# Graph layer with a sort on chip: five VectorE operations a sort stage, one stream of sort slots over three walks, sixteen one-hots and eight gather slots

## The reference, cut to what matters

```python
x   = x + gnn(layernorm(x), W, row=src, col=dst, vals=edge_weight)
x   = x + ffn(layernorm(x), W_ffn, b_ffn)
# gnn: h = x @ W.T ; out[row[e]] += vals[e] * h[col[e]]   for 131,072 edges
```

## Time and profile before

| | us |
|---|---|
| median of 3 runs (1778.59 to 1779.0) | 1778.88 |
| the profiled execution's own time | 1777.97 |
| its span, first to last instruction | 1776.2 |
| phase 1 / four walks / rest, cut at the first and the last gather | 278 / 1331 / 167 |
| busy in the whole span: PE, DVE, ACT, POOL | 1633.4, 1173.2, 604.1, 1065.1 |

### The profile page before, as it was taken

The page is one execution under the profiler, slowest core; times in us unless marked ns, Lnnn a source line. Parts: engine busy times, 40 slices in busy tenths (PEclk is TensorE's granted clock), DMA queues, the critical chain, the costliest instruction groups (busy, mean ns, idle before and its releaser), DMA issues.

```text
span 1776.2 us, 29342 instructions
## 1 busy us (share of the span) xinstructions
PE 1633.4 (92%) x4076; PEld 651.5 (37%) x4077; DVE 1173.2 (66%) x4540; ACT 604.1 (34%) x1354; POOL 1065.1 (60%) x1114
## 2 busy tenths in 40 slices
PE   7999997999999999999999999999999999995995
PEld 4455542433333423333333233333343333332442
DVE  7666656777777787778777877878743333335465
ACT  7777732222222222222222122222244444443341
POOL 1000005777777777777667677776777777775930
PEclk9999998999999999999999999999999999998798
DMA  7334215777777777766667676766677777772334
GB/s 256 119 133 136 91 68 167 212 209 207 209 206 207 209 207 204 203 198 196 191 191 202 189 202 192 203 193 188 192 209 210 209 209 210 210 209 64 131 111 140
DMA packets 121766, 323.92 MB, mean 182 GB/s; under 512 B 20434, under 2 KB 39154, under 8 KB 121586
## 3 DMA queue, kind: packets, MB, share of 16 engines
q0 software_dynamic: 81920, 268.50, 53.2%
q1 hardware_dynamic: 39666, 53.48, 8.9%
HBM read 288.35 MB, written 33.55 MB: 181 GB/s over the span
## 4 chain that ended last, share of the span: by engine, by line
PE 55%; DVE 16%; DMA 9%; issue 8%; POOL 7%; DVEq 3%; ACT 1%; SPq 1%; ACTq 0%; POOLq 0%
PE psum L1201 34%; PE psum L1109 12%; DMA region<-h_rows,region 9%; POOL region L519 7%; DVE region L918 5%; PE psum L1280 4%; DVEq L918 2%; DVE region L827 2%; DVE region L817 2%; PE psum L1098 2%; DVE region L821 1%; DVE region L829 1%; DVE region L831 1%; DVE region L823 1%; PE psum L1248 1%
## 5 line engine op out<-in xcount | busy, mean ns | idle before, releaser
L519 POOL DMA_INDIRECT region<-h_rows,region x1024 | 984.8, 962 | 615.9 <-DMA h_rows<-region 268.8
L1201 PE MATMUL psum<-region 128*128 x2552 | 1237.3, 617 | 84.2 <-DVE region L918 44.8
L1201 PEld LDWEIGHTS psum<-region 128*128 128x128 f32 x2552 | 433.3, 189 | 849.9 <-issue 845.7
L918 DVE SCALAR_TENSOR_TENSOR region<-region 128x128 f32 (+1 forms) x1276 | 450.5, 353 | 437.8 <-PE psum L1201 290.7
L679 ACT ACTIVATE x<-psum 128x512 f32<-128x512 f32 x192 | 114.6, 597 | 784.8 <-PE psum L1201 784.8
L1109 PE MATMUL psum<-region 128*128 128x512 f32 x512 | 230.2, 593 | 0.8 <-ACT region L581 0.8
L831 DVE COPY_PREDICATED region<-region 128x128 f32<-128x128 int32 x452 | 159.0, 352 | 0.0
L827 DVE COPY_PREDICATED region<-region 128x128 f32<-128x128 int32 x452 | 158.1, 350 | 0.0
L662 ACT ACTIVATE psum<-x 128x512 f32<-128x512 f32 x256 | 153.7, 601 | 8.0
L817 DVE TENSOR_TENSOR region<-region 128x128 int32<-128x128 f32 x452 | 130.4, 289 | 23.1 <-ACT region L608 21.5
L829 DVE TENSOR_TENSOR region<-region 128x128 f32<-128x128 f32 x452 | 136.4, 302 | 0.0
(11 more groups left out here) (150 smaller groups left out, 637.9 us busy)
## 6 DMA issues: line engine op xcount, KB each, us to landing
x<-in_x SPq DMA_DIRECT2D x16, 1024.0 KB, 6.1
h_rows<-region SPq DMA_DIRECT2D x64, 256.0 KB, 2.0
region<-h_rows,region POOLq DMA_INDIRECT x1024, 3.7
out<-x SPq DMA_DIRECT2D x4, 2816.0 KB, 10.8
out<-x SPq DMA_DIRECT2D x8, 640.0 KB, 3.4
region<-in_L_gnn_weight SPq DMA_DIRECT2D x1, 1024.0 KB, 5.5
region<-in_src SPq DMA_DIRECT2D x4, 128.0 KB, 2.5
region<-in_dst SPq DMA_DIRECT2D x4, 128.0 KB, 2.4
```

The source lines that it names most:

```text
L519: pool.indirect_dma_start(gathered[:, (c + 1) % RING, :], None, h_dram, bass.IndirectOffsetOnAxis(ap=dst_i[g][:, i:i + 1], axis=0),).then_ ...
L918: dve.scalar_tensor_tensor(spread[:, slot % SR, :], iota_n[:, bass.ds((tile - (g * T + 1)) * P, P)], src_f[g][:, bass.ds(chunk - (g * NC + ...
L1201: pe.matmul(banks[:, bass.ds(pe.snap(tile_wanted) % AGG, 1), :].rearrange("p t f -> p (t f)"), spread[:, slot % SR, :], gathered[:, bass.d ...
```

## The change

- A stage has five operations. Weights now alternate between two buffers too, `other_weights` and `weight[g]`. In the keys slot, **all** weights (256 columns) are copied to the other buffer in place of the low half, between compare and minimum. The weights slot is the maximum, then **one** predicated copy of 256 columns: mask broadcast over both halves, data read with the halves of each pair exchanged.
- "pack" copies the part's weights into `other_weights` first (one operation more).
- Where VectorE moves turned data (not ScalarE), only the keys are copied from PSUM. The first stage behind the turn reads the weights from PSUM directly; TensorE no longer waits for a copy of them.
- `plan()` has 0.65 for a keys and for a weights slot, before 0.6 and 0.85. Worked through, `HEAD` goes from slot 40 (17 whole stages of part 1) to slot 59 (26 stages), and every one of the 18 turns and sums of part 0 moves one tile of phase 1 earlier (the first from behind tile 9 to behind tile 8, with the same spacings after it).
- What is left of parts 1 to 3 is one list, spread evenly over steps 0 to 944 of 957; before, each walk had its own. A stage (keys 1.0, weights 0.9) gets 2.08 steps in every walk; before 2.16 in walk 0 and 1.91 in walks 1 and 2.
- `SR` 8 to 16, `RING` 11 to 8.

```diff
-    RING = 11
-    SR = 8
+    RING = 8
+    SR = 16
@@ plan
-        vector_times = {"pack": 6.0, "flip": 0.3, "keys": 0.6, "weights": 0.85, ...
+        vector_times = {"pack": 6.0, "flip": 0.3, "keys": 0.65, "weights": 0.65, ...
@@ slots_with_steps
+        left = [(g, slot) for g in range(1, PARTS) for slot in SORT_SLOTS[HEAD if g == 1 else 0:]]
+            return {"keys": 1.0, "weights": 0.9, "turned": 0.9, "flip": 0.4, "rest": 0.5}.get(what, 0.7)
+        room = ((PARTS - 1) * NS - LAST_STEPS) / sum(shares)
@@ sort_edges
+                        dve.tensor_copy(weights_now, weight[g]).then_inc(s_sort[g], 1)
...
-                        dve.tensor_copy(kept, low_w).then_inc(s_sort[g], 1)
+                        dve.tensor_copy(weights[1 - now], weights_now).then_inc(s_sort[g], 1)
                         dve.wait_ge(s_sort[g], done + 1)
                         dve.tensor_tensor(to_low, low, high, ALU.min).then_inc(s_sort[g], 1)
...
-                        dve.copy_predicated(low_w, swap, high_w).then_inc(s_sort[g], 1)
-                        dve.wait_ge(s_sort[g], done)
                         dve.tensor_tensor(to_high, low, high, ALU.max).then_inc(s_sort[g], 1)
-                        dve.wait_ge(s_sort[g], done + 1)
-                        dve.copy_predicated(high_w, swap, kept).then_inc(s_sort[g], 1)
+                        dve.wait_ge(s_sort[g], done)
+                        dve.copy_predicated(both(weights[1 - now], j),
+                                            swap.unsqueeze(2).to_broadcast(both(weights_now, j).shape),
+                                            both(weights_now, j)[:, :, ::-1, :]).then_inc(s_sort[g], 1)
...
-                            dve.tensor_copy(keys[now], turned_keys).then_inc(s_key_in[g], 1)
-                            dve.wait_ge(s_turn_w[g], turns)
-                            dve.tensor_copy(weight[g], turned_weights).then_inc(s_wgt_in[g], 1)
+                            weights_now = turned_weights
+                            dve.wait_ge(s_turn_k[g], turns)
+                            dve.tensor_copy(keys_now, turned_keys).then_inc(s_key_in[g], 1)
+                            dve.wait_ge(s_key_in[g], turns)
```

More of the change, by code:

```diff
@@ L101, in gnn_ffn @@
     assert sum(what == "turn" for what, _, _ in SORT_SLOTS) == TURNS
+    assert sum(what == "weights" for what, _, _ in SORT_SLOTS) % 2 == 1
     def plan():
-        vector_times = {"pack": 6.0, "flip": 0.3, "keys": 0.6, "weights": 0.85, "turned": 1.9, "maxima": 2.5,
+        vector_times = {"pack": 6.0, "flip": 0.3, "keys": 0.65, "weights": 0.65, "turned": 1.9, "maxima": 2.5,
                         "counts": 2.0, "rows": 2.0, "index": 0.4, "source": 0.8}
@@ L135, in gnn_ffn, with slots_with_steps, share @@
     HEAD_TURNS = sum(what == "turn" for what, _, _ in SORT_SLOTS[:HEAD])
[L137 to L145, removed]
+    def slots_with_steps():
+        left = [(g, slot) for g in range(1, PARTS) for slot in SORT_SLOTS[HEAD if g == 1 else 0:]]
+        def share(what):
+            return {"keys": 1.0, "weights": 0.9, "turned": 0.9, "flip": 0.4, "rest": 0.5}.get(what, 0.7)
+        shares = [share(what) for _, (what, _, _) in left]
+        room = ((PARTS - 1) * NS - LAST_STEPS) / sum(shares)
+        found, at = [0] * (PARTS * NS), 0.0
+        for (g, _), of_one in zip(left, shares):
+            step = int(at * room)
+            assert step < g * NS - LAST_STEPS
+            found[step] += 1
+            at += of_one
         return found
@@ L165, in gnn_ffn @@
         AT_SORT = AT_DATA + PARTS * 3 * NC
[L166 removed]
+        AT_TAB = AT_SORT + 4 * NC
         REGION = AT_TAB + NSP + NC + T
@@ L204, in gnn_ffn @@
         keys = [carve(NC), carve(NC)]
-        rest = carve(NC + NC // 2)
+        rest = carve(2 * NC)
         swaps = [rest[:, i * NC // 2:(i + 1) * NC // 2].bitcast(I32) for i in range(2)]
-        low_kept = rest[:, NC:NC + NC // 2]
-        below = low_kept
+        other_weights = rest[:, NC:2 * NC]
+        below = other_weights[:, 0:NC // P * T]
         over = rest[0:T, 0:NSP]
@@ L372, in row_of, with weights_of @@
             return slice(32 * g, 32 * g + 1)
-        SORT_STEPS = {"pack": 2, "flip": 1, "keys": 3, "weights": 3}
+        SORT_STEPS = {"pack": 3, "flip": 1, "keys": 3, "weights": 2}
+        BY_SCALAR = (TURNS, HEAD_TURNS) + (0,) * (PARTS - 2)
+        def weights_of(g):
+            return other_weights, weight[g]
         def progress(turn):
@@ L768, in sort_edges, with both @@
                 done = turns = now = half = 0
+                weights = weights_of(g)
+                keys_now, weights_now = keys[0], weights[0]
+                def both(a, j):
+                    return a.rearrange("p (b s d) -> p b s d", s=2, d=1 << (j if j < 7 else j - 7))
                 def pairs(a, j):
-                    v = a.rearrange("p (b s d) -> p b s d", s=2, d=1 << (j if j < 7 else j - 7))
-                    return v[:, :, 0, :], v[:, :, 1, :]
+                    return both(a, j)[:, :, 0, :], both(a, j)[:, :, 1, :]
                 def single(a, j):
@@ L810, in sort_edges @@
                     elif what == "keys":
-                        low, high = pairs(keys[now], j)
+                        low, high = pairs(keys_now, j)
                         to_low, to_high = pairs(keys[1 - now], j)
-                        low_w, high_w = pairs(weight[g], j)
                         swap = single(swaps[half], j)
-                        kept = single(low_kept, j)
                         dve.wait_ge(s_sort[g], done - 1)
                         dve.tensor_tensor(swap, low, high, ALU.is_gt).then_inc(s_sort[g], 1)
-                        if turns:
+                        if turns > BY_SCALAR[g]:
+                            dve.wait_ge(s_turn_w[g], turns)
+                        elif turns:
                             dve.wait_ge(s_wgt_in[g], turns)
                         dve.wait_ge(s_sort[g], done)
-                        dve.tensor_copy(kept, low_w).then_inc(s_sort[g], 1)
+                        dve.tensor_copy(weights[1 - now], weights_now).then_inc(s_sort[g], 1)
                         dve.wait_ge(s_sort[g], done + 1)
@@ L925, in _ @@
                 dve.wait_ge(s_hst[u], 16 * (T // 4))
[L926 to L934, removed]
+            following = chain(second, *[sort_edges(g) for g in range(2, PARTS)])
+            for at, slots in enumerate(slots_with_steps()):
+                build(*divmod(at, NS))
+                for _ in range(slots):
+                    next(following)
+                if at == SR:
+                    for cleared in (all_fwT, all_fw_in, bias.rearrange("p h l -> p (h l)"), fw_out[:, :]):
+                        dve.memset(cleared, 0.0).then_inc(s_fz, 1)
             go, = counters(dve, "dve_live")
@@ L1115, in turn_edges @@
                 pe.wait_ge(s_sort[g], steps - 1)
-                if turn or g:
-                    pe.wait_ge(s_key_in[g if turn else g - 1], turn if turn else TURNS)
+                if 0 < turn <= BY_SCALAR[g]:
+                    pe.wait_ge(s_key_in[g], turn)
                 for b in range(NC // P):
@@ L1121, in turn_edges @@
                 pe.wait_ge(s_sort[g], steps)
-                if turn or g:
-                    pe.wait_ge(s_wgt_in[g if turn else g - 1], turn if turn else TURNS)
+                if 0 < turn <= BY_SCALAR[g]:
+                    pe.wait_ge(s_wgt_in[g], turn)
                 for b in range(NC // P):
-                    last = pe.transpose(bank(WEIGHT_BANK)[:, b * P:(b + 1) * P], weight[g][:, b * P:(b + 1) * P], ident[:, :])
+                    last = pe.transpose(bank(WEIGHT_BANK)[:, b * P:(b + 1) * P],
+                                        weights_of(g)[buffer][:, b * P:(b + 1) * P], ident[:, :])
                 last.then_inc(s_turn_w[g], 1)
@@ L1204, in add_step @@
                           start=False, stop=True, skip_group_check=True).then_inc(s_done, 1)
[L1206 to L1211, removed]
+            following = chain.from_iterable(((g, what) for what, _, _ in SORT_SLOTS[HEAD if g == 1 else 0:])
+                                            for g in range(1, PARTS))
+            for at, slots in enumerate(slots_with_steps()):
+                add_step(*divmod(at, NS))
+                for of_part, what in islice(following, slots):
+                    of_sort(of_part, what)
             assert turned == [TURNS] * PARTS
```

14 lines of the change are left out of this document (8 added, 6 removed).

## The result

| | before | after |
|---|---|---|
| median of 13 runs each, us | 1779.0 | 1772.9 |
| ratio (95% interval) | | 0.995 (0.993 to 0.997) |
| profiled execution: its time / span, us | 1777.97 / 1776.2 | 1774.97 / 1773.1 |
| phase 1 / walks 0 to 3 / rest, us | 278.0 / 325.4, 339.5, 345.1, 321.0 / 167.2 | 277.6 / 334.6, 333.7, 332.7, 320.9 / 173.6 |

One of the 13 runs after took 1811.8 us, far from the other twelve (1768.0 to 1777.1), and is left out of the ratio. Faster by 0.5%, where 1.4% was forecast: the sign is right, the size is not. The walks together lost 9.1 us.

What follows compares the result with a forecast made beforehand. It took GpSimd to bound walks 0 and 3, VectorE walks 1 and 2. Walks 0 to 2 -33.8, gathers +4.5, slots +3, phase 1 +2: -24.3 us, giving 1754.6 us, range 1737 to 1782.

Steps and rivals of the forecast that it cites:

- The bounds before: Walks of the kernel before: GpSimd bounds walks 0 and 3, VectorE walks 1 and 2, which lose 14.1 and 19.7 us.
- VectorE's need: VectorE's time for a whole part, sort and one-hots: falls from 342.3 to 326.0 us, with 0.12 saved a stage.
- The wide predicated copy's 0.34: Weights slot: the predicated copy of 256 columns lets its successor start after 0.34 us.
- its cover under the register work: Where a one-hot follows the predicated copy, its register work needs 0.40 us anyhow, hiding 0.14 us.
- The wider copy and GpSimd: Gathers in the walks slow beside the stage's longer copy: 1.5 us more a walk, +4.5 (bounds 0 and +9.6).
- Eight slots: RING 11 to 8 in the walks: slack falls from 6.7 to 2.9 us, costing +3 for all three parts.
- Phase 1: Before the first turn, one tile earlier, TensorE waits 1.5 to 3 us for VectorE: +2 (bounds 0 and +5).
- B: Rival in the walks: too few gather slots, GpSimd waits at register loads and turns; about 1773 us, chance 0.15.
- C: Rival: TensorE's own work, never VectorE, held walks 1 and 2; 1781 us, chance 0.07.
- D: Rival in the stage: the wide predicated copy is dearer than the two it replaces; about 1797 us, chance 0.11.

Runs made afterwards that it cites:

- e3: Kernel before with only the change's plan times and single stream of sort slots, old six-operation stage, 11 gather slots, 8 one-hots: 1765.5 us, ratio 0.990.
- e9: Kernel before with the change's sort slots; only the first stage behind a VectorE turn uses a wide predicated copy, reading PSUM: 1754.7 us, ratio 0.987.
- e13: e9 with plan times 0.6 and 0.6 and a longer HEAD of 94: 1749.8 us, ratio 0.981 (second run).
- e12: Changed kernel with the stage's copy cut to one column and the predicated copy to the low halves, weights wrong: 1741.6 us (second run).
- e1: Changed kernel with the stage's copy of all weights cut to one column, weights wrong: 1754.8 us, ratio 0.984.
- e2: Changed kernel with the weights copy within SBUF made by a minimum of the weights with themselves: 1826.3 us, ratio 1.025.
- e4: Changed kernel with 10 gather slots and 8 one-hots instead of 8 and 16: 1773.0 us, ratio 0.994.
- e8: e3 with 8 gather slots and 16 one-hots: 1769.9 us, ratio 0.994.
- e5: Changed kernel with the stage's copy of 256 weights made as two copies of 128: 1828.1 us, ratio 1.027.
- e11: e3 with one more copy of 128 weights in the keys slot, ahead of the stage's copy: 1772.3 us, one run.
- e10: Changed kernel with the minimum moved from the keys slot to the head of the weights slot: 1759.7 us, ratio 0.987.

## Why the prediction was off, point by point

- **The bounds before: right.** VectorE in walks 1 and 2, GpSimd in 0 and 3. e3 and e9 lower walks 1 and 2 with VectorE's need, to 334 and then 329 to 331, and e13 and e12 end at 324 to 325, GpSimd's pace.
- **VectorE's need: right in kind, too high.** The wide predicated copy's 0.34 and its cover under the register work held; a stage with its two one-hots fell by 0.28 us, not 0.12, as the one-hot behind the minimum comes 0.38 instead of 0.46 later and the one behind the predicated copy 0.34 instead of 0.40. It changed nothing in the walks, as VectorE has over 100 us to spare. (HEAD 40 ends within a stage, behind its minimum, the operation at 248.71 in the earlier trace rows: 16 stages and a keys slot before, 25 and a keys slot after, where I counted 17 and 26. That is worth half a microsecond.)
- **The failed step: "The wider copy and GpSimd", +4.5 us (bounds 0 and +9.6).** It scaled the narrow operations' 12 ns a gather with the copy's duration and looked at the copy alone. (By its own numbers the scaling gives 3.2 x (0.29 / 0.22 - 1) = 1.0 us a walk, not the 1.5 that it states; the slip is small beside the miss.) Measured: the 768 gathers of walks 0 to 2 took 766.9 us against 740.6 before and 739.7 in e12, some 27 us. The walks took 1001.0 where 976.2 + 4.5 + 3 = 983.7 were forecast, 17.3 over: 24.8 us from the gathers in place of 4.5, nothing from the slots in place of 3. Beside a one-column copy (e1 against e12) 11 us go with the wide predicated copy, which the term left out. The rows of before could hardly show it: beside the copies from PSUM they hold only 13 VectorE operations on 256 columns of SBUF in the three walks, where the change puts two into nearly every stage.

  The Trainium skill's page "SBUF — State Buffer" ("SBUF: two separate sides") says that a VectorE copy in a two-port mode and a GpSimd operation shut each other out for a whole instruction, and so does a VectorE operation with two SBUF inputs, but only against a GpSimd operation that reads SBUF. The traces agree in kind: lengthened gathers end 0.82 us behind the end of a VectorE operation, and in e2 the operation with two SBUF inputs is as bad; a gather does read its row numbers from SBUF. They do not show the size: its 2.5 us for one copy is not seen, the longest gather here had 0.8 us on top, and the kernel before, whose copies and two-input operations are of 128 columns, has no gather above 1.17 us. I had put the rule aside on the size and should have kept its mechanism as a rival with a price of its own.
- **Eight slots: +3 forecast, 0 measured in the change** (e4), 4 us where VectorE is near the bound (e8).
- **Phase 1: +2 forecast, -0.4 measured.** The forecast took the old stage's pace up to the first turn. TensorE did it at 50.61 us without a wait for VectorE, whose last operation of that stage had started at 48.98, where it was 51.56 before. With the old stage (e3) the wait is there, 0.77 us at 51.42, and phase 1 takes 279.2.
- **The rivals.** Neither too few slots (B) nor TensorE (C) nor a dear predicated copy (D). The time fell near B's 1773 for a reason not on the list: GpSimd's gaps stayed at 0.30 us, and its gathers grew.

**Left open.** Why a gather is held over a whole run of operations in the new stage, and slips in behind the compare of an old one; why two narrow copies (e5) do what a wide one does, though the same number in e11 doesn't; and what sets the place at which VectorE's steps settle against the gathers. A version with wide operations in which VectorE never waits was not tried.

## What to carry to other kernels

When an engine's work is made cheaper by moving more in fewer operations, look at what the other engines do beside it: here the saving went to an engine that was not the bound any more, and the new operations slowed the one that was. Test a compound change in halves; the slots alone gave twice what the whole gave, and the operation that did the harm could be kept where it read PSUM. A mean duration over all instances (0.964 against 0.999) nearly hides this; the maximum and the count above a limit show it.

## What was not expected of the hardware

- A gather's issue on GpSimd went from 0.95 us to as much as 1.76 beside a run of VectorE operations (compare, two copies, minimum in e5; minimum, maximum, wide predicated copy in e10), depending on where within some 0.3 us it started. It then ended 0.80 to 0.82 us behind the end of the run.
- Work on VectorE between a sort operation and a one-hot is free up to its register work: in the walks a second copy in each of 313 stages cost nothing (e11).
- The same kernel took 1779 us and, on one chip, 2004 us; with e13 the gathers there moved 177 GB/s, elsewhere 208 to 210.
